# A graph kernel: counts rounded to 16 bits by GpSimd and turned as 16-bit blocks, and another order of VectorE's work behind attention

## The chip, the cores and the metric

The kernel runs on one core of a Trainium2 chip. The metric is the device time of one execution in microseconds; the median of several runs counts. Five engines work side by side, each through its own list of instructions: TensorE (PE in the profile, with its weight loads as PEld), VectorE (DVE), ScalarE (ACT), GpSimd (POOL) and SyncE (SP), which here only issues transfers. They wait for each other through semaphores.

## The reference

1250 nodes with 512 features, 21250 edges. Two layers, each behind a layer norm and a ReLU, each added to its input:

```
h = max(layernorm(x), 0);  x = x + attention(h)
h = max(layernorm(x), 0);  x = x + experts(h)

attention:  h = nodes @ W + b_w
            e = leaky_relu(s_dst[dst] + s_src[src] + b_a, 0.2);  w = exp(e)
            out[n] = sum over edges into n of w / (sum of w) * h[src]
experts:    gates = softmax(x @ gate_W + gate_b);  the top 2 of 4 experts of each node
            each expert: twice  h = relu((mean of h over neighbours) @ Wl + bl + h @ Wr)
            out = sum over the two of gate * expert output
```

## The kernel before

**Counts.** The graph is turned into a dense matrix of counts first: `CT[:, t, n]` (125 x 10 x 1250, 32-bit) says how many edges go from source node (t, p) to target node n. It is made on TensorE from one-hot rows in ten batches; `windows_out` copies it from PSUM. In the last layer of the experts the same counts are needed by target node, as 16-bit numbers in DRAM (`c_d`), from which GpSimd gathers rows. So the kernel turns every block of CT once.

**Attention.** It runs over `QN` = 5 blocks of 250 target nodes, and in each over `NP` = 5 pairs of the T = 10 source tiles; pair g = 5 q + j. For each pair VectorE makes the arguments (`arguments`, `z_l`), ScalarE the exponentials (`z_e`), VectorE multiplies them by the counts (`weights`, `p_f`), ScalarE copies the high part (`p_hi`), and VectorE adds `p_f` to the running sum (`sum_up`) and subtracts for the low part (`weights_low`, `p_lo`). RA = 3 pairs are in flight. TensorE takes each source tile s with six matmuls of 512 columns (two target tiles, three products of high and low parts, function `three`), and waits for `p_lo` ahead of each pair. At the end of a block `weight_sums` sums the weights, and VectorE's `attended` divides, adds the input and takes the row statistics. VectorE's order of instructions is written out by hand.

**Turning.** `turn_counts(q, r)`, r = 0 to 5, turns four, four and two blocks of 125 x 125 for each of the two target tiles, behind source tiles s = 2 to 7 of its block. ScalarE's `counts_out` copies the turned blocks as 16-bit numbers into `c_16`, with the row sums as a by-product (`deg_part`, the degrees), and SyncE stores `c_16`. A flag `beyond`, read into a register, says that a count may be over 2048; then the part that 16 bits lose is kept as well. With these inputs it is 0, and the parts under `If(beyond)` are skipped.

**Behind attention.** The second layer norm (`norm2`, `h2_f`), its split into `nat_hi` and `nat_lo`, its transposes (`turn2`, `h2T_hi`, `h2T_lo`), the gate logits, and `neighbours1`: the sum over neighbours, which for row tile t multiplies `CT_hi[:, t]` (a cast of CT) by the high and the low part of that tile. The first two row tiles have their high and low parts in `nat_a`. From t = 2 on TensorE waits for `nat_lo` of tile t, which `rows_low(t)` makes on VectorE.

**GpSimd** builds constants in the first 10 us and then has nothing to do until the second layer's neighbour sums are done.

Of the kernel before, what the change touches and what calls it, by code (L numbers as in the profile page):

```python
# [37 lines left out]
def gnn_kernel(nc, x, src, dst, W0, b_w, a_vec, b_a, gate_W, gate_b, Wl, bl, Wr, out):  # L38
# [37 lines left out]
    with ctx:  # L76
# [4 lines left out]
        def at(name, shape, dt, offset):  # L81
            return nc.alloc_sbuf_tensor_at(name, shape, dt, offset=origin + offset)
# [146 lines left out]
        nat_a = at("nat_a", [P, 2, 2, D], F32R, R3 + 30528)  # L229
        assert R3 + 30528 + 8192 <= R4  # L230
        ag1 = at("ag1", [P, 4, D], F32, R4 + 8192)
        c_nat = at("c_nat", [P, 2, N], F32, R3 + 20480)
        c_16 = at("c_16", [P, 2, N], F16, R3 + 10240)
        c_lo = at("c_lo", [P, 2, N], F16, R3 + 15264)


        slots = at("slots", [128, 2, 18432], F32R, 0)
# [72 lines left out]
        def signals(names, start=0):  # L310
            return [Signal(ctx.enter_context(nc.semaphore(n)), start) for n in names.split()]
# [3 lines left out]
            "pad_ready spark_ready edges_in x_in x_late_in w0_in vec_in small_in gw_in ct_out x2_out rest_in")  # L315

        c_turned, c_nat_ready = signals("c_turned c_nat_ready")
        LOW_READY, LOW_OUT = 2 * (N // Q), 16
        (c_out,) = signals("c_out", 64)

# [79 lines left out]

        def counts_beyond(eng):

            eng.wait_ge(*flag_ready(1))
# [3 lines left out]
            return beyond  # L407

        def apart(eng):

# [14 lines left out]
        QN = N // Q  # L425
        CONSTS = 8
        TURNS = (4, 4, 2)
        CUTS = (slice(0, 112), slice(112, P))
        AGG = ((0, 4, 3, 1, 2), (9, 8, 5, 6, 7))
        AGG_BANK = {0: 0, 1: 1, 2: 2, 3: 3, 4: 4, 9: 3, 8: 4, 5: 5, 6: 6, 7: 7}  # L430
# [27 lines left out]
        def _(sp):  # L458
# [18 lines left out]
            for q in range(QN):  # L477
                for i in range(2):
                    n = q * Q + i * P
                    sp.wait_ge(*c_nat_ready(6 * q + 3 * i + 3))  # L480
                    for m in CUTS:
                        sp.dma_start(c_d[n + m.start:n + m.stop, :], c_16[m, i, :]).then_inc(c_out.sem, 16)
                    with sp.If(beyond_sp):
                        if q == i == 0:
                            sp.wait_ge(*ct_out(LOW_OUT))
                        sp.wait_ge(*rest_ready(2 * q + i + 1))
                        for m in CUTS:
                            sp.dma_start(cl_d[n + m.start:n + m.stop, :], c_lo[m, i, :]).then_inc(ct_out.sem, 16)

            sp.wait_ge(*x2_ready(T))  # L490
            for m in CUTS:
# [70 lines left out]
        def _(pool):  # L562
# [43 lines left out]
            with pool.If(beyond):  # L606
                for q in range(QN):
                    for i in range(2):
                        pool.wait_ge(*c_nat_ready(6 * q + 3 * i + 3))
                        if q > 0:  # L610
                            pool.wait_ge(*ct_out(LOW_OUT, 64 * q))
                        g.tensor_tensor(c_lo[:, i, :], c_nat[:, i, :], c_16[:, i, :], ALU.subtract
                                        ).then_inc(rest_ready.sem, 1)
            with pool.If(beyond):
                pool.wait_ge(*ct_out(16))
# [88 lines left out]
        def _(act):  # L704
# [98 lines left out]
                bias_in(b)  # L803
                windows_out(b)

            beyond = counts_beyond(act)

            def row_out(k):
                act.wait_ge(*sd_spread(k + 1))
# [26 lines left out]
            def counts_out(q, r):  # L836
                n = TURNS[r % 3]
                act.wait_ge(*c_turned(q * 6 + r + 1))
                if r == 0 and q > 0:
                    act.wait_ge(*c_out(0, q * 64))  # L840
                to, turned = slice(r % 3 * 4 * P, (r % 3 * 4 + n) * P), ps[0:P, 6 + r % 2, 0:n * P]
                with act.If(beyond):
                    if r == 0 and q > 0:
                        act.wait_ge(*rest_ready(2 * q))
                    copy(c_nat[:, r // 3, to], turned)
                a.activation(c_16[:, r // 3, to], turned, ACT.Copy,
                             accum_out=deg_part[:, q * 6 + r:q * 6 + r + 1]).then_inc(c_nat_ready.sem, 1)

            def root(k, n):
                act.wait_ge(*var2_ready(k + 1))  # L850
# [11 lines left out]
            for g in range(NP * QN + 3):  # L862
                if g < NP * QN:
                    exponentials(g)
                if 1 <= g <= NP * QN:
                    weights_high(g - 1)
                if g == 1:
                    product_high(T - 1)
                if g in (2, 8):
                    row_out({2: 1, 8: 2}[g])  # L870
                for q in range(QN):
                    for r in range(6):
                        if NP * q + (r + 2) // 2 + 3 == g:
# [16 lines left out]
            for t in range(T):  # L890
                if t == 2:
                    act.wait_ge(*p_used(NP * QN))
                if t >= 2:
                    rows_high(t)
                if t == 3:
                    root(1, slice(T - 2, T))
                if t + 2 == 5:
# [139 lines left out]
        def _(dve):  # L1037
# [198 lines left out]
            dve.wait_ge(*flag_ready(1))  # L1236
            for b in range(T):
                tile_and_batch(b)
                if b == T - 1:
# [132 lines left out]
                    "p (c n) -> p c n", n=P), f32(h2T_hi[:, :, t * P:(t + 1) * P]), ALU.subtract  # L1372
                                ).then_inc(h2T_lo_ready.sem, 1)

            attended(QN - 1)
# [9 lines left out]
            def rows_low(t):  # L1385
                dve.wait_ge(*h2_hi_ready((t - 2) % T + 1))
                v.tensor_tensor(nat_lo[:, t, :], h2_f[:, t, :], f32(nat_hi[:, t, :]), ALU.subtract
                                ).then_inc(h2_lo_ready.sem, 1)
# [232 lines left out]
        def _(pe):  # L1621
# [165 lines left out]
            def turn_counts(q, r):  # L1787

                n = TURNS[r % 3]
                if q == 0 and r == 1:  # L1790
                    pe.wait_ge(*row_ready(2))
                pe.wait_ge(*c_nat_ready(q * 6 + max(r - 1, 0)))
                for k in range(n):
                    t = r % 3 * 4 + k
                    last = nc.tensor.transpose(ps[0:P, 6 + r % 2, k * P:(k + 1) * P],  # L1795
                                               CT[:, t, q * Q + r // 3 * P:q * Q + r // 3 * P + P], ident[0:P, 0:P])
                last.then_inc(c_turned.sem, 1)

            def weighted_sums(q):
                for j in range(NP):  # L1800
# [5 lines left out]
                    for m in range(2):  # L1806
# [85 lines left out]
            beyond = counts_beyond(pe)  # L1892
            turn2(0)
            turn2(1)
            for t in range(T):
# [194 lines left out]
```

## Time and profile before

| | |
|---|---|
| median of 3 runs | 774.83 us (774.81 to 775.18) |
| profiled execution | 777.36 us, span of the profile 775.3 us |
| PE busy | 745.5 us, 96% of the span |
| PEld, DVE, ACT, POOL busy | 605.7, 395.0, 278.9, 120.3 us |
| chain that ended last | PE 91%, DVE 5%, ACT 2%, issue 1% |

The stages: one-hot rows and counts to about 108 us, attention from 108 to 197, second layer norm and neighbour sums to 261, the experts' first layer to 488, and the second, for gathered rows, to the end. A row of a time line gives the start and the length in us, the engine, the line, the operation, what is written and read, how many instructions it covers, and in brackets the idle time before it and what ended it. The length of a pipelined instruction is longer than the step to the next one; steps between starts say what one costs in a stream.

### The profile page before, as it was taken

Reading aid. Unit: us, or ns where it says so; the run is one execution under the profiler, and the core shown is the slowest. Engines: PE = TensorE matmul, PEld = TensorE weight load, DVE = VectorE, ACT = ScalarE, POOL = GpSimd, SP = SyncE. Lnnn points to the kernel's source line nnn. Section 1 sums busy time; section 2 is a strip of 40 time slices with the busy share of each in tenths; the row PEclk is TensorE's granted clock in tenths of the full one; section 3 lists DMA queues with packets and bytes.
Section 4 is the critical chain, followed back from the end, with each engine's and each line's share of the span. In section 5 each row is a group of like instructions: output and inputs, shape, how many; then the busy total and the mean of one; then the engine's idle time right before and its main releaser. Section 6 shows DMA issues by size and latency. Waiting matters only on the chain.

```text
span 775.3 us, 11763 instructions
## 1 busy us (share of the span) xinstructions
PE 745.5 (96%) x3746; PEld 605.7 (78%) x3746; DVE 395.0 (51%) x979; ACT 278.9 (36%) x577; POOL 120.3 (16%) x133
## 2 busy tenths in 40 slices
PE   5899989999999999999999999899999999999994
PEld 3589968888788887777777777788887888888883
DVE  8898998997742549423525324333323323323320
ACT  6966675655543523312314213122122212211211
POOL 4000000000000103720000100231332322322211
PEclk9999999999999999999999999999999999999997
DMA  9000001111401447799696873599427944349800
GB/s 216 20 4 4 4 1 34 33 50 34 148 2 55 126 130 244 210 347 323 248 358 241 302 283 86 155 274 321 89 53 221 341 123 87 75 101 283 293 11 6
DMA packets 45319, 115.09 MB, mean 148 GB/s; under 512 B 7300, under 2 KB 7432, under 8 KB 45241
## 3 DMA queue, kind: packets, MB, share of 16 engines
q1 hardware_dynamic: 28581, 77.60, 30.7%
q0 software_dynamic: 8016, 19.59, 11.0%
q10 hardware_dynamic: 8644, 16.86, 6.5%
q8 instruction: 48, 0.79, 0.4%
q14 instruction: 30, 0.25, 0.1%
HBM read 64.85 MB, written 50.07 MB: 148 GB/s over the span
## 4 chain that ended last, share of the span: by engine, by line
PE 91%; DVE 5%; ACT 2%; issue 1%; POOL 0%; DVEq 0%; ACTq 0%; POOLq 0%
PE ps L1629 18%; PE ps L1630 18%; PE ps L1631 18%; PE ps L2021 7%; PE ps L2020 6%; PE ps L1706 3%; PE ps L1878 3%; PE ps L1879 3%; PE ps L1942 2%; PE ps L2031 1%; PE ps L1986 1%; PE ps L1795 1%; PE ps L1767 1%; PE ps L1657 1%; PE ps L1769 1%; PE ps L1768 1%
## 5 line engine op out<-in xcount | busy, mean ns | idle before, releaser
L2021 PE MATMUL ps<-slots,CTs 125*128 x230 | 91.2, 396 | 0.0
L2020 PE MATMUL ps<-slots,CTs 125*128 x207 | 81.5, 394 | 0.0
L1460 DVE TENSOR_TENSOR he_t<-ps,b_b 125x512 f32<-125x512 f32 x40 | 27.6, 691 | 102.5 <-PE ps L1631 70.9
L964 ACT ACTIVATE slots<-he_t 125x512 fp32r<-125x512 f32 x40 | 25.3, 635 | 148.4 <-DVE he_t L1460 141.6
L1553 DVE CAST CTs<-ps 125x512 fp32r<-125x512 f16 (+1 forms) x69 | 37.3, 595 | 76.5 <-PE ps L1942 72.8
L671 POOL DMA_INDIRECT out<-tg,rec x23 | 37.1, 1613 | 182.5 <-ACT tg L1014 159.0
L1629 PE MATMUL ps<-W,agT_hi 128*125 128x512 f32 x160 | 63.5, 397 | 0.0
L1629 PE MATMUL ps<-W,h2T_hi 128*125 128x512 f32 x160 | 63.4, 396 | 0.0
L1631 PE MATMUL ps<-W,agT_lo 128*125 128x512 f32 x160 | 63.3, 396 | 0.0
L1630 PE MATMUL ps<-W,agT_hi 128*125 128x512 f32 x160 | 63.2, 395 | 0.0
L1630 PE MATMUL ps<-W,h2T_hi 128*125 128x512 f32 x160 | 63.2, 395 | 0.0
L1631 PE MATMUL ps<-W,h2T_lo 128*125 128x512 f32 x160 | 63.1, 394 | 0.0
L1599 DVE TENSOR_TENSOR tm<-ps,b_b 128x512 f32<-128x512 f32 x23 | 15.9, 692 | 81.9 <-PE ps L1631 81.9
L1199 DVE TENSOR_SCALAR onehot_g<-iota_h,column 125x250 bf16<-125x250 f16 x250 | 49.7, 281 | 6.0 <-PE ps L1706 4.6
L1007 ACT ACTIVATE heT<-ps 128x512 fp32r<-128x512 f32 x23 | 13.8, 599 | 107.3 <-PE ps L1986 102.7
L2021 PEld LDWEIGHTS ps<-slots,CTs 125*128 125x128 f32 x230 | 43.3, 188 | 9.8
L2020 PEld LDWEIGHTS ps<-slots,CTs 125*128 125x128 f32 x207 | 38.9, 188 | 8.9
L1629 PE MATMUL ps<-nat_hi,p_hi 125*125 125x512 f32 x100 | 42.4, 424 | 2.4 <-issue 2.0
L1018 ACT ACTIVATE agn<-ps,rec 128x512 f32<-128x512 f32 x23 | 15.8, 688 | 79.4 <-PE ps L2021 79.4
L1629 PE MATMUL ps<-slots,heT 128*128 x92 | 40.0, 435 | 0.1
L1630 PE MATMUL ps<-nat_lo,p_hi 125*125 125x512 f32 x100 | 39.6, 396 | 0.0
L1631 PE MATMUL ps<-nat_hi,p_lo 125*125 125x512 f32 x100 | 39.5, 395 | 0.0
(299 smaller groups left out, 1666.9 us busy)
## 6 DMA issues: line engine op xcount, KB each, us to landing
he_d<-slots SPq DMA_DIRECT2D x30, 448.0 KB
slots<-he_d SPq DMA_DIRECT2D x30, 448.0 KB
w_d<-slots SPq DMA_DIRECT2D x3, 4096.0 KB, 17.4
slots<-w_d SPq DMA_DIRECT2D x24, 512.0 KB
t_d<-he_t SPq DMA_DIRECT2D x40, 224.0 KB
raw<-in_L_gnn_Wl ACTq DMA_DIRECT2D x4, 1024.0 KB, 9.0
raw<-in_L_gnn_Wr ACTq DMA_DIRECT2D x4, 1024.0 KB, 5.6
slots<-in_L_gnn_Wl ACTq DMA_DIRECT2D x4, 1024.0 KB, 10.0
```

The source lines that it names most:

```text
L671: g.indirect_dma_start(out, bass.IndirectOffsetOnAxis(ap=i32(rec[:, i, 2:3]), axis=0), tg[i % 3][:], None, bounds_check=N - 1, oob_is_err= ...
L964: a.activation(HE[:, t, 0:D], he_t[:, (x * T + t) % 4, :], ACT.Relu).then_inc(he_hi_ready.sem, 1)
L1199: last = v.tensor_scalar(onehot_g[:, k, j, :], iota_h[:], column[:, b % 2 * BW + k, j:j + 1], None, ALU.is_equal)
L1460: v.tensor_tensor(he_t[:, n % 4, :], ps[0:P, bank_of(x, g, t), :], b1_b[:, x % 2, :], ALU.add).then_inc(pre_ready.sem, 1)
L1553: v.tensor_copy(CTs[:, 4 * r:4 * r + n, :], turned_counts(r, n)).then_inc(cts_ready.sem, 1)
L1629: mm(o, l_hi, r_hi, start=start, stop=False)
L1630: mm(o, l_hi, r_lo, start=False, stop=False)
L1631: return mm(o, l_lo, r_hi, start=False, stop=stop)
L1706: last = mm(ps[0:P, k, 0:WT], onehot_p[:, bass.ds(first + j, 1), :].rearrange("p o n -> p (o n)"), onehot_g[:, slot, j, :], start=opens an ...
L1878: mm(o, count, hi, start=t == 0, stop=False)
L2020: mm(o, CTs[:, t, :], part(k, P, t * 1024, P), start=False, stop=False)
L2021: last = mm(o, CTs[:, t, :], part(k, P, t * 1024 + D, P), start=False, stop=t == T - 1)
```

## The change

GpSimd casts the counts of each block of 250 target nodes to 16 bits: `ct_16[q % 2]`, 125 x 10 x 250, once the counts are complete and the first layer's product of the last tile is done (the place in memory was that of the first layer's weights). Block q + 1 is cast after block q; from block 2 on the cast waits until the block that had its buffer is turned. It also casts a 16-bit identity, `ident_a`. TensorE turns the 16-bit blocks into 16-bit PSUM; ScalarE copies them to `c_16`. The 32-bit way stays for the case `beyond`, and a second flag, `usual`, selects the new way; TensorE and ScalarE read both into registers. In block 0 the turns move two source tiles back (`TURN_FROM`). Some tiles move in memory; the wait of ScalarE for the stored `c_16` moves one row tile back.

Behind attention VectorE makes the gate weights' low part, `CT_hi` and `nat_lo` of row tile 2 and `h2T_lo` of tile 1 ahead of the statistics of the last two tiles and of the degrees.

```diff
+        ct_16 = [at(f"ct_16_{k}", [P, T, Q], F16, R3 + 4096 + 5024 * k) for k in range(2)]
+        ident_a = at("ident_a", [P, P], F16, R2 + 39328)
...
+        TURN_FROM = (4, 2)
...
@@ GpSimd
+            pool.wait_ge(*batch_done(T))
+            g.tensor_copy(ident_a[:], ident[0:P, 0:P]).then_inc(consts.sem, 1)
+            pool.wait_ge(*window_out(NW))
+            pool.wait_ge(*hw_done(T))
+
+            def counts_16(q):
+                if q > 1:
+                    pool.wait_ge(*c_turned(6 * (q - 1)))
+                g.tensor_copy(ct_16[q % 2][:], CT[:, :, q * Q:(q + 1) * Q]).then_inc(ct_16_ready.sem, 1)
+
+            counts_16(0)
+            for q in range(QN):
+                if q + 1 < QN:
+                    counts_16(q + 1)
+                with pool.If(beyond):
...
@@ ScalarE, counts_out
-                a.activation(c_16[:, r // 3, to], turned, ACT.Copy,
-                             accum_out=deg_part[:, q * 6 + r:q * 6 + r + 1]).then_inc(c_nat_ready.sem, 1)
+                with act.If(usual):
+                    a.activation(c_16[:, r // 3, to].rearrange("p (t n) -> p t n", n=P),
+                                 ps_h[0:P, 6 + r % 2, 0:n * S].rearrange("p (t n) -> p t n", n=S)[:, :, 0:P], ACT.Copy,
+                                 accum_out=deg_part[:, q * 6 + r:q * 6 + r + 1]).then_inc(c_nat_ready.sem, 1)
...
-                        if NP * q + (r + 2) // 2 + 3 == g:
+                        if NP * q + (r + TURN_FROM[q > 0]) // 2 + 3 == g:
...
@@ VectorE
+            v.tensor_scalar(flag_i[:, 1:2], fl_f[:, 1:2], EXACT, None, ALU.is_le).then_inc(flag_ready.sem, 1)
...
             attended(QN - 1)
             turned_low2(0)
+            dve.wait_ge(*gw_hi_ready(1))
+            v.tensor_tensor(gw[:, :, NE:], gw_f[:], f32(gw[:, :, 0:NE]), ALU.subtract).then_inc(gw_lo_ready.sem, 1)
+            counts_high(2)
+            rows_low(2)
+            turned_low2(1)
             dve.wait_ge(*stats_ready(T))
             normed(1, late)
-            dve.wait_ge(*gw_hi_ready(1))
-            v.tensor_tensor(gw[:, :, NE:], gw_f[:], f32(gw[:, :, 0:NE]), ALU.subtract).then_inc(gw_lo_ready.sem, 1)
...
-            for t in range(T):
-                if t >= 2:
+            for t in range(1, T):
+                if t >= 3:
                     rows_low(t)
...
-                if t > 0:
+                if t > 1:
                     turned_low2(t)
...
@@ TensorE, turn_counts
+                if r == 0:
+                    pe.wait_ge(*ct_16_ready(q + 1))
...
+                with pe.If(usual):
+                    for k in range(n):
+                        t = r % 3 * 4 + k
+                        last = nc.tensor.transpose(ps_h[0:P, 6 + r % 2, k * S:k * S + P],
+                                                   ct_16[q % 2][:, t, r // 3 * P:(r // 3 + 1) * P], ident_a[:])
+                    last.then_inc(c_turned.sem, 1)
+                with pe.If(beyond):
...
-                        if T - 8 <= s < T - 2:
-                            turn_counts(q, s - (T - 8))
+                        if TURN_FROM[q > 0] <= s < TURN_FROM[q > 0] + 6:
+                            turn_counts(q, s - TURN_FROM[q > 0])
```

## Rows read from the trace of the kernel before

**Rows 1.** TensorE's waits from 100 to 330 us: us in all, times, longest.

```profile
PE ps L1629 <- issue: 2.0, 1, 2.0
PE ps L1878 <- DVE nat_lo L1387: 0.9, 1, 0.9
PE ps L1629 <- DVE p_lo L1313: 0.4, 1, 0.4
```

**Rows 2.** Time line of TensorE around a group of four 32-bit transposes, attention.

```profile
115.98 0.60 PE L1795 MATMUL ps<-ident,CT 125*125 125x125 f32 x4
...
116.66 0.40 PE L1630 MATMUL ps<-nat_lo,p_hi 125*125 125x512 f32 x1
116.89 0.39 PE L1631 MATMUL ps<-nat_hi,p_lo 125*125 125x512 f32 x1
```

**Rows 3.** The same around ten 16-bit transposes, last layer; a skipped conditional precedes them.

```profile
568.36 0.39 PE L2021 MATMUL ps<-slots,CTs 125*128 x1
568.59 0.74 PE L1942 MATMUL ps<-ident_h,crow 128*125 128x128 f16 x10
...
569.45 0.39 PE L1630 MATMUL ps<-slots,heT 128*128 x1
```

**Rows 4.** Time line of attention's last block, VectorE and TensorE.

```profile
186.14 0.68 DVE L1313 TENSOR_TENSOR p_lo<-p_f,p_hi 125x500 fp32r<-125x500 f32 x1
...
186.87 0.49 PE L1629 MATMUL ps<-nat_hi,p_hi 125*125 125x512 f32 x1
```

**Rows 5.** Time line of VectorE behind attention.

```profile
200.95 0.66 DVE L1371 TENSOR_TENSOR h2T_lo<-ps,h2T_hi 128x500 fp32r<-128x500 f32 x1
...
202.63 1.53 DVE L1358 CAST CT_hi<-CT 125x1250 fp32r<-125x1250 f32 x2
```

**Rows 6.** Stretches: length, busy us of PE, PEld, DVE, ACT, POOL, granted clock, DMA.

```profile
206.00:208.00 2.00, 2.00 (x7) 1.55 (x6) 1.97 (x6) 0.27 (x1) 0.00 (x0) 0.58 0.93 295
```

**Rows 7.** Time line of TensorE behind attention, rounds of row tiles 2 and 3.

```profile
203.82 0.65 PE L1839 MATMUL ps<-ident,h_f 125*128 125x125 f32 x4
205.40 0.50 PE L1878 MATMUL ps<-nat_hi,CT_hi 125*125 125x512 f32 x1 [0.94 <-DVE nat_lo L1387]
...
210.19 0.65 PE L1839 MATMUL ps<-ident,h_f 125*128 125x125 f32 x4
210.59 0.48 PE L1878 MATMUL ps<-nat_hi,CT_hi 125*125 125x512 f32 x1
...
213.79 0.64 PE L1839 MATMUL ps<-ident,h_f 125*128 125x125 f32 x4
```

**Rows 8.** GpSimd's groups of instructions by form: busy us, mean ns.

```profile
L600 POOL CAST iota_h<-iota_i 125x250 f16<-125x250 int32 x1 | 0.4, 394 | 0.1
...
L632 POOL CAST tile_f<-tile_i 125x24 f32<-125x24 int32 x1 | 0.2, 204 | 0.1
```

**Rows 9.** Time line of GpSimd and then VectorE at 262 us.

```profile
262.59 0.30 POOL L629 TENSOR_SCALAR_AFFINE_SELECT before_p<-before_p 125x125 f32<-125x125 f32 x1
...
262.59 0.31 DVE L1441 TENSOR_TENSOR cmp<-lg 125x10 f32<-125x10 f32 x1
...
263.23 0.18 DVE L1441 TENSOR_TENSOR cmp<-lg 125x10 f32<-125x10 f32 x1
```

**Rows 10.** Time line of VectorE and then GpSimd at 7 us.

```profile
6.69 0.93 DVE L1067 SCALAR_TENSOR_TENSOR e_q<-e_t,e_src 32x750 fp32r<-32x750 f32 x1
...
7.08 0.63 POOL L593 TENSOR_SCALAR_AFFINE_SELECT tri<-tri 50x50 f32<-50x50 f32 x1
```

**Rows 11.** Time line of VectorE at attention's start.

```profile
108.32 0.68 DVE L1294 SCALAR_TENSOR_TENSOR p_f<-z_e,CT 125x500 f32<-125x500 f32 x1 [0.27 <-ACT z_e L824]
```

**Rows 12.** A stretch of one block of attention, columns as in rows 6.

```profile
146.34:163.34 17.00, 17.00 (x89) 14.18 (x89) 15.45 (x32) 10.03 (x27) 0.00 (x0) 1.00 0.12 37
```

**Rows 13.** Time line of block 2, VectorE and TensorE.

```profile
151.40 0.67 DVE L1313 TENSOR_TENSOR p_lo<-p_f,p_hi 125x500 fp32r<-125x500 f32 x1
...
152.59 0.48 PE L1629 MATMUL ps<-nat_hi,p_hi 125*125 125x512 f32 x1
```

More of the change, by code:

```diff
@@ L228, in gnn_kernel @@
         rest = at("rest", [P, T, P], F32R, row_at)
-        nat_a = at("nat_a", [P, 2, 2, D], F32R, R3 + 30528)
-        assert R3 + 30528 + 8192 <= R4
+        nat_a = at("nat_a", [P, 2, 2, D], F32R, R3 + 31808)
+        assert R3 + 31808 + 8192 <= R4
         ag1 = at("ag1", [P, 4, D], F32, R4 + 8192)
-        c_nat = at("c_nat", [P, 2, N], F32, R3 + 20480)
-        c_16 = at("c_16", [P, 2, N], F16, R3 + 10240)
-        c_lo = at("c_lo", [P, 2, N], F16, R3 + 15264)
+        c_nat = at("c_nat", [P, 2, N], F32, R3 + 21760)
+        ct_16 = [at(f"ct_16_{k}", [P, T, Q], F16, R3 + 4096 + 5024 * k) for k in range(2)]
+        c_16 = at("c_16", [P, 2, N], F16, R3 + 14144)
+        c_lo = at("c_lo", [P, N], F16, R3 + 19168)
+        ident_a = at("ident_a", [P, P], F16, R2 + 39328)
         slots = at("slots", [128, 2, 18432], F32R, 0)
@@ L317, in gnn_kernel @@
         c_turned, c_nat_ready = signals("c_turned c_nat_ready")
+        (ct_16_ready,) = signals("ct_16_ready")
         LOW_READY, LOW_OUT = 2 * (N // Q), 16
@@ L401, in counts_beyond @@
         def counts_beyond(eng):
-            eng.wait_ge(*flag_ready(1))
+            eng.wait_ge(*flag_ready(2))
             _, (beyond,) = nc.values_load_multi_w_load_instructions(
@@ L407, in counts_beyond, with counts_within @@
             return beyond
+        def counts_within(eng):
+            eng.wait_ge(*flag_ready(2))
+            _, (usual,) = nc.values_load_multi_w_load_instructions(
+                flag_i[0:1, 1:2], engines=[eng.engine], min_val=0, max_val=1,
+                skip_runtime_bounds_check_because="it is 0 or 1")
+            return usual
         def apart(eng):
@@ L487, in _ @@
                         for m in CUTS:
-                            sp.dma_start(cl_d[n + m.start:n + m.stop, :], c_lo[m, i, :]).then_inc(ct_out.sem, 16)
+                            sp.dma_start(cl_d[n + m.start:n + m.stop, :], c_lo[m, :]).then_inc(ct_out.sem, 16)
             sp.wait_ge(*x2_ready(T))
@@ L605, in _ @@
             beyond = counts_beyond(pool)
-            with pool.If(beyond):
-                for q in range(QN):
+            pool.wait_ge(*batch_done(T))
[11 more added lines that the diff above has]
+                with pool.If(beyond):
                     for i in range(2):
                         pool.wait_ge(*c_nat_ready(6 * q + 3 * i + 3))
-                        if q > 0:
-                            pool.wait_ge(*ct_out(LOW_OUT, 64 * q))
-                        g.tensor_tensor(c_lo[:, i, :], c_nat[:, i, :], c_16[:, i, :], ALU.subtract
+                        if q + i > 0:
+                            pool.wait_ge(*ct_out(LOW_OUT, 64 * q + 32 * i))
+                        g.tensor_tensor(c_lo[:], c_nat[:, i, :], c_16[:, i, :], ALU.subtract
                                         ).then_inc(rest_ready.sem, 1)
@@ L804, in _ @@
                 windows_out(b)
-            beyond = counts_beyond(act)
+            beyond, usual = counts_beyond(act), counts_within(act)
             def row_out(k):
@@ L845, in counts_out @@
                     copy(c_nat[:, r // 3, to], turned)
-                a.activation(c_16[:, r // 3, to], turned, ACT.Copy,
-                             accum_out=deg_part[:, q * 6 + r:q * 6 + r + 1]).then_inc(c_nat_ready.sem, 1)
+                    a.activation(c_16[:, r // 3, to], turned, ACT.Copy,
+                                 accum_out=deg_part[:, q * 6 + r:q * 6 + r + 1]).then_inc(c_nat_ready.sem, 1)
+                with act.If(usual):
+                    a.activation(c_16[:, r // 3, to].rearrange("p (t n) -> p t n", n=P),
+                                 ps_h[0:P, 6 + r % 2, 0:n * S].rearrange("p (t n) -> p t n", n=S)[:, :, 0:P], ACT.Copy,
+                                 accum_out=deg_part[:, q * 6 + r:q * 6 + r + 1]).then_inc(c_nat_ready.sem, 1)
             def root(k, n):
@@ L896, in _ @@
                     root(1, slice(T - 2, T))
-                if t + 2 == 5:
+                if t + 2 == 6:
                     act.wait_ge(*c_out(64 * QN))
@@ L1234, in spread_out @@
                                 ).then_inc(sd_ready.sem, 1)
-            dve.wait_ge(*flag_ready(1))
+            dve.wait_ge(*flag_ready(2))
             for b in range(T):
@@ L1373, in turned_low2, with rows_low @@
                                 ).then_inc(h2T_lo_ready.sem, 1)
+            def rows_low(t):
+                dve.wait_ge(*h2_hi_ready((t - 2) % T + 1))
+                v.tensor_tensor(nat_lo[:, t, :], h2_f[:, t, :], f32(nat_hi[:, t, :]), ALU.subtract
+                                ).then_inc(h2_lo_ready.sem, 1)
             attended(QN - 1)
             turned_low2(0)
+            dve.wait_ge(*gw_hi_ready(1))
[3 more added lines that the diff above has]
+            turned_low2(1)
             dve.wait_ge(*stats_ready(T))
             normed(1, late)
-            dve.wait_ge(*gw_hi_ready(1))
-            v.tensor_tensor(gw[:, :, NE:], gw_f[:], f32(gw[:, :, 0:NE]), ALU.subtract).then_inc(gw_lo_ready.sem, 1)
             dve.wait_ge(*c_nat_ready(6 * QN))
@@ L1384, in _ @@
             link(v.reciprocal(inv_deg[:], inv_deg[:]))
[L1385 to L1388, printed above, removed]
-            for t in range(T):
-                if t >= 2:
+            for t in range(1, T):
+                if t >= 3:
                     rows_low(t)
@@ L1792, in turn_counts @@
                 pe.wait_ge(*c_nat_ready(q * 6 + max(r - 1, 0)))
[L1793 to L1797, printed above, removed]
+                if r == 0:
+                    pe.wait_ge(*ct_16_ready(q + 1))
+                    if q == 0:
+                        pe.wait_ge(*consts(CONSTS + 1))
+                with pe.If(usual):
[5 more added lines that the diff above has]
+                with pe.If(beyond):
+                    for k in range(n):
+                        t = r % 3 * 4 + k
+                        last = nc.tensor.transpose(ps[0:P, 6 + r % 2, k * P:(k + 1) * P],
+                                                   CT[:, t, q * Q + r // 3 * P:q * Q + r // 3 * P + P], ident[0:P, 0:P])
+                    last.then_inc(c_turned.sem, 1)
             def weighted_sums(q):
@@ L1815, in weighted_sums @@
                             last.then_inc(p_used.sem, 1)
-                        if T - 8 <= s < T - 2:
-                            turn_counts(q, s - (T - 8))
+                        if TURN_FROM[q > 0] <= s < TURN_FROM[q > 0] + 6:
+                            turn_counts(q, s - TURN_FROM[q > 0])
+            beyond, usual = counts_beyond(pe), counts_within(pe)
             pe.wait_ge(*window_out(NW))
@@ L1890, in turn_means1 @@
                 last.then_inc(ag1_turned.sem, 1)
-            beyond = counts_beyond(pe)
             turn2(0)
```

## The prediction

> **What bounds the kernel now.** I read the page's busy shares first, then TensorE's list of waits, then the time line around the change. TensorE is the bound: from 100 to 330 us it waits three times, 3.3 us in all [rows 1]: 2.0 us before attention's first product (the weights of the first source tiles are not ready), 0.4 us before the second pair of source tiles, and 0.9 us for the third row tile's low part (`nat_lo`). So what leaves TensorE's stream there comes off the end, and what makes VectorE late at one of these places goes onto it. Behind 330 us its stream has almost no gaps, and its loads are triggered by its own progress; I take it that it shifts as a whole.
>
> **Part 1, the 100 transposes.** Attention turns 20 blocks of counts in each of five blocks of target nodes. A group of four 32-bit transposes starts at 115.98, and the second matmul behind it at 116.66, where one matmul steps by 0.23: 0.68 - 0.23 = 0.45 us, 112 ns each [rows 2]. Ten 16-bit transposes of nearly the same shape, in the last layer: 569.45 - 568.59 - 0.23 = 0.63 us, 63 ns each [rows 3]. I take 48 ns saved (bounds: 37, if entering a group costs 0.08 us of the 0.63 and groups of four and two pay it as often as they come, and 55, if it costs nothing and 125 columns are cheaper than 128), so 0.95 us per block and 4.75 in all. Two groups of four in the last block give nothing: there TensorE already waits for VectorE (the low part ends at 186.82, the product starts at 186.87) [rows 4]; that is 8 x 0.048 = 0.4 less. ScalarE gets one more conditional between a turned block and its copy, on the chain that leads to the second layer norm; I take 0.15 us there (0 to 0.5). Sum: -4.2 us.
>
> The conditionals on TensorE, two per group, I cost at nothing: one stands just ahead of the ten transposes at 568.59, and the step over it is the usual 0.23 [rows 3]. Their cover is the queue of matmuls before them. The two registers that TensorE now reads before attention lie in its 2 us wait, and ScalarE's lies beside its copies of the last windows.
>
> **Part 2, VectorE's new order.** The sequence after attention is h2T_lo of tile 0, statistics, gate weights, degrees, two `CT_hi`, h2T_lo of tile 1, `nat_lo` of tile 2. The first of these ends at about 201.6, and two casts, 0.77 us each, start at 202.63 [rows 5], so 1.0 us of small work, a second cast and an h2T_lo (0.66) stood ahead of `nat_lo`. In the new order only the gate weights, one cast and `nat_lo` stand there: 201.6 + 0.1 + 0.8 + 0.7 = 203.2. TensorE's transposes start at 203.82, and it goes on 0.4 later, as from 210.19 to 210.59 [rows 7], so it needs it at 204.2. The 0.94 us wait goes. The moved work is late for nobody: the degrees are used only by the means at this stage's end, the square root of the last two tiles waits on ScalarE behind other work anyway, and row tile 3's low part, followed through the new order in the same way, comes 0.5 us before its need.
> The wait has a second price. The granted clock was 0.58 from 206 to 208 [rows 6], that is half speed (1.2 GHz) for most of it, after the pause; and one round, from one set of transposes to the next, took 210.19 - 203.82 = 6.37 us where the next took 213.79 - 210.19 = 3.60 [rows 7]. Both together are 2.8 us. I take all of it: other rounds have the same small matmuls without the wait and keep their clock. Bound: 0.9 if the clock falls anyway.
>
> **Part 3, GpSimd's five casts and VectorE.** Before, GpSimd does nothing in this stage. Now it casts 125 x 2500 numbers five times. Length: 24 columns took 0.204 us and 250 took 0.394 [rows 8], 0.84 ns a column, so 0.18 + 2500 x 0.00084 = 2.3 us; the upper bound is ten casts of 250, 3.9 us. The first cast ends by 111.2, and TensorE needs it behind 30 matmuls of block 0, 7 us after it starts on them: it doesn't wait for it.
> VectorE does. At 262.59 GpSimd's select (0.30 us, reading SBUF) and VectorE's 10-column comparison of two SBUF inputs start together; the comparison takes 0.31 and ends when the select ends, where the same one takes 0.18 at 263.23 [rows 9]. And at 7.08 a GpSimd select of 50 columns, behind a VectorE instruction with two SBUF inputs that runs to 7.62, takes 0.63 [rows 10]; GpSimd gets in behind that one instruction, though VectorE has more to do. So each shuts the other out, and GpSimd gets its turn. All of attention's VectorE work but the normalisation of finished rows has two SBUF inputs. The rows show this only for operations of 0.3 us. The lower bound is no hold beyond that, 5 x 0.13 = 0.7 us, the upper one the whole length; I take the whole length, since in both pairs the held one ended only when the other did.
> The Trainium skill (SBUF — State Buffer, Who interferes with whom) says that a VectorE instruction with two SBUF inputs and a GpSimd one that reads SBUF exclude each other for the whole instruction. The rows agree, for short ones. By that rule the sum is the one below; by what the rows show of duration alone, it would be the lower bound's.
>
> Where it lands: (a) the start. Casts 0 and 1 follow each other once the last product is out, at about 108.3, just as VectorE starts its first weights [rows 11] in the chain that TensorE waits for. One VectorE instruction may slip between them; the chain is 2 x 2.25 = 4.5 us later, and so is TensorE's first product. It has then been idle for 2.0 + 4.5 = 6.5 us. After the 0.94 us pause it went to half speed, after the 2.0 us one not; I take it that it does here. The low clock cost 2.8 - 0.94 = 1.8 us of the one round at most; here 0.4 of it is free, in the wait for the second pair of tiles. I take 0.9 (0 to 1.4). Start: +5.4 us (0.5 to 5.9 at this cast length).
> (b) Cast 2 waits for block 0's last turn; VectorE then has only normalisation to do, which reads PSUM: 0.
> (c) Casts 3 and 4 start after the last turn of blocks 1 and 2, when VectorE isn't through. It is busy 15.45 us of a block's 17.0 [rows 12]; with a block of 16.05 there are 0.6 us left, so it comes 2.3 - 0.6 = 1.7 us late to the next block. The low part of its third pair of tiles was done at about 152.0, TensorE took them up at 152.59 [rows 13]: a cushion of 0.6, less the 8 x 0.048 = 0.4 by which TensorE now comes earlier. TensorE waits 1.7 - 0.2 = 1.5 us, twice: +2.9. What is queued behind VectorE's held instruction is the sum and low part of the last pair and then the next block's normalisation; TensorE waits for none of them, but for what follows.
> The small cast of the identity (0.3 us, near 104) costs VectorE up to 0.25 us that its wait for `row` at 106 covers.
>
> **Sum.** -4.2 - 2.8 + 5.4 + 2.9 = +1.3 us. The profiled execution took 777.36 us over a span of 775.3; it would become 778.7 and 776.6. The median of the three runs is 774.83, 2.5 less, and the change is added to that: 776.1.
>
> **Rivals.**
> - *They share.* GpSimd holds VectorE for about half of its length (bursts, or it yields). Start 2.5, blocks 0.5: -7.0 + 3.0 = -4.0, 770.8 us. For it: no row shows a hold over 0.3 us. Against: the held one always ended with the holder.
> - *No hold worth speaking of.* -7.0 and at most +0.7: 768.1 us. Against it: the two pairs of rows.
> - *Slower, by one thing: a longer cast.* Ten separate rows of 250 at 3.9 us. Start 2 x 3.85 + 0.9 = 8.6, blocks 2 x (3.9 - 0.6 - 0.2) = 6.2, less 7.0: +7.8, 782.6 us. Each 0.1 us of a cast costs 0.4 us; above 2.4 us the change is slower by more than can be told from nothing. For it: GpSimd's own rows are of 250 columns at most. Against: its time grows evenly with the columns.
> - *The new order gives only 0.9*, since the clock falls anyway: +1.9 on any of these. The rounds after it speak against it.
>
> **How the numbers follow.** A measurement of this kernel can tell about 0.2%, 1.55 us, from no change. The full hold has 0.55, and gives 776.1 with its own range of 773.5 to 778.5; of this, slower 0.24, same 0.29, faster 0.02. Sharing has 0.25 (faster 0.21, same 0.04), no hold 0.12 (faster), the longer cast 0.08 (slower). Together: faster 0.35, same 0.33, slower 0.32. The range leaves out the 0.12 below and the longer cast above: 769.5 to 779.0.
>
> **What the profile after would show.** The 100 transposes in groups of 0.25 us instead of 0.45; no wait for `nat_lo` and a granted clock of 1.00 from 206 to 210; GpSimd's casts of 2.3 us with VectorE starting nothing with two SBUF inputs beside them; TensorE's wait before attention 6.5 instead of 2.0 us, and new waits for `p_lo` of some 1.5 us in blocks 2 and 3. The prediction is wrong if VectorE's instructions run beside the casts, if a cast takes far from 2.3 us, or if TensorE's wait at the start is still 2 us.

## The result: 777.5 us, 0.3% slower

The changed kernel took 777.47 us (median of 8 runs, 776.97 to 777.59), the kernel before beside it 774.87 us (8 runs, 774.24 to 775.98). The ratio is 1.0031, 95% interval 1.0020 to 1.0041: slower by 2.4 us by the ratio and by 2.6 us by the medians, and clear of no change. Forecast were 776.1 us and a range from 769.5 to 779.0. The profiled execution took 777.35 us over a span of 775.2.

TensorE's waits from 100 to 330 us in the changed kernel (against [rows 1]):

```profile
PE ps L1662 <- issue: 6.1, 1, 6.1
PE ps L1662 <- DVE p_lo L1343: 1.7, 3, 0.8
```

The wait at the start has grown from 2.0 to 6.1 us, those for `p_lo` from 0.4 to 1.7, and the wait for `nat_lo` is gone. Who makes the start late stands in the time lines of GpSimd, VectorE and TensorE at attention's start (against [rows 8] and [rows 11]):

```profile
108.37 5.21 POOL L626 CAST ct<-CT 125x2500 f16<-125x2500 f32 x2 [3.91 <-PE ps L1802]
...
108.36 0.68 DVE L1324 SCALAR_TENSOR_TENSOR p_f<-z_e,CT 125x500 f32<-125x500 f32 x1 [0.26 <-ACT z_e L849]
108.95 4.89 DVE L1307 SCALAR_TENSOR_TENSOR z_l<-row,s_rest,row_low 125x250 f32<-125x250 f32 x2
113.77 0.67 DVE L1324 SCALAR_TENSOR_TENSOR p_f<-z_e,CT 125x500 f32<-125x500 f32 x1
...
115.13 0.76 PE L1662 MATMUL ps<-nat_hi,p_hi 125*125 125x512 f32 x1 [6.06 <-issue]
115.69 0.63 PE L1663 MATMUL ps<-nat_lo,p_hi 125*125 125x512 f32 x1
```

In the kernel before the same two `z_l` are:

```profile
108.92 0.86 DVE L1277 SCALAR_TENSOR_TENSOR z_l<-row,s_rest,row_low 125x250 f32<-125x250 f32 x2
```

They take 4.89 us beside two casts instead of 0.86, 4.03 us more. By VectorE's list of that tile one `z_l` took 2.50 us at most and 0.47 in the median: each of the two is held by one cast, and the first slips in before the second cast. TensorE then runs at half speed (a matmul of 512 columns steps by 0.42 us instead of 0.23; the granted clock is 0.50 from 116 to 117 us).

The 16-bit transposes in TensorE's stream, a group of four and one of two (against [rows 2]):

```profile
123.78 0.39 PE L1833 MATMUL ps<-ident_a,ct 125*125 125x125 f16 x4
123.98 0.47 PE L1662 MATMUL ps<-nat_hi,p_hi 125*125 125x512 f32 x1
124.29 0.39 PE L1663 MATMUL ps<-nat_lo,p_hi 125*125 125x512 f32 x1
...
127.14 0.28 PE L1833 MATMUL ps<-ident_a,ct 125*125 125x125 f16 x2
127.22 0.48 PE L1662 MATMUL ps<-nat_hi,p_hi 125*125 125x512 f32 x1
127.54 0.40 PE L1663 MATMUL ps<-nat_lo,p_hi 125*125 125x512 f32 x1
```

By the reckoning of [rows 2]: 124.29 - 123.78 - 0.23 = 0.28 us for four, 0.17 for two. Four were 0.45. VectorE beside block 3's cast (146.32 to 148.94 us), the two waits of TensorE behind such casts, and the stretch from block 1's denominators to block 2's (against [rows 12]):

```profile
146.32 2.88 DVE L1307 SCALAR_TENSOR_TENSOR z_l<-row,s_rest,row_low 125x250 f32<-125x250 f32 x2
...
156.67 0.50 PE L1662 MATMUL ps<-nat_hi,p_hi 125*125 125x512 f32 x1 [0.59 <-DVE p_lo L1343]
...
173.95 0.50 PE L1662 MATMUL ps<-nat_hi,p_hi 125*125 125x512 f32 x1 [0.78 <-DVE p_lo L1343]
```

```profile
148.95:166.02 17.07, 16.48 (x89) 13.23 (x88) 17.00 (x32) 10.14 (x27) 2.41 (x1) 1.00 0.12 38
```

VectorE is busy for 17.00 of 17.07 us, where it had 1.55 us of slack. The stretch holds block 4's cast (2.41 us), so part of the 17.00 is time in which VectorE is held. Behind attention, the place of [rows 7] and of [rows 6]:

```profile
207.26 0.65 PE L1884 MATMUL ps<-ident,h_f 125*128 125x125 f32 x4
207.67 0.48 PE L1923 MATMUL ps<-nat_hi,CT_hi 125*125 125x512 f32 x1
...
210.86 0.65 PE L1884 MATMUL ps<-ident,h_f 125*128 125x125 f32 x4
```

```profile
206.00:208.00 2.00, 2.00 (x17) 1.85 (x16) 1.90 (x9) 0.05 (x1) 0.00 (x0) 1.00 1.00 317
```

One round takes 3.60 us, no wait, full clock, as forecast. Yet the profiled spans of the two kernels are equal (775.3 and 775.2), and the medians are 2.6 us apart. So before any cause is named, the first profile of the kernel before has to be looked at again.

### The profile page after: what moved, and what is told of

The parts are those of the page before. It is cut to its first block, busy times and chain, and to the rows that moved or that the text cites. A ratio compares the mean times of both kernels' runs of the same rounds, so it can differ in the third digit from the quotient of the medians.

```text
span 775.2 us, 11871 instructions
## 1 busy us (share of the span) xinstructions
PE 741.5 (96%) x3746; PEld 601.6 (78%) x3746; DVE 402.3 (52%) x980; ACT 278.9 (36%) x577; POOL 133.6 (17%) x139
## 4 chain that ended last, share of the span: by engine, by line
PE 90%; DVE 6%; issue 2%; ACT 1%; POOL 0%; DVEq 0%; ACTq 0%; POOLq 0%
PE ps L1662 18%; PE ps L1663 17%; PE ps L1664 17%; PE ps L2065 7%; PE ps L2064 6%; PE ps L1739 3%; PE ps L1923 3%; PE ps L1924 3%; PE ps L1986 2%; PE ps L2075 1%; PE ps L2030 1%; PE ps L1800 1%; PE ps L1802 1%; PE ps L1801 1%; PE ps L1690 1%
## 5 line engine op out<-in xcount | busy, mean ns | idle before, releaser
L681 POOL DMA_INDIRECT crow<-c_d,rec x23 | 22.7, 985 | 103.1 <-DVE W L1461 96.4
```

## The experiments

All are measured against the kernel before on the same chip. The casts are numbered 0 to 4 by the block whose counts they make.

### The kernel before, once more

> The kernel before, once more, for its profile. The first profile of it lasted 777.36 us where its runs have a median of 774.9. Theory one: the low granted clock behind attention (206 to 210 us there, some 1.8 us) isn't in most executions, so this profile has a span of about 773 us and a granted clock of 1.00 from 206 to 208. Theory two: the episode is in every execution, and the 2.5 us lie elsewhere: span 773 us too, but with the episode. Ratio to itself 1.000.

774.69 us against 774.54, ratio 1.0009 (0.9998 to 1.0020). That is the resolution. The new profile has a span of 772.8 us, 2.5 less than the first one. Its stretches at 206 and at 495 us, then those of the first profile:

```profile
206.00:208.00 2.00, 2.00 (x12) 1.62 (x11) 1.97 (x6) 0.32 (x1) 0.00 (x0) 1.00 0.94 294
495.00:500.00 5.00, 5.00 (x16) 3.75 (x16) 0.78 (x2) 0.60 (x1) 2.59 (x3) 0.66 0.77 211
```

```profile
495.00:500.00 5.00, 3.44 (x11) 2.82 (x11) 0.69 (x1) 0.58 (x1) 3.82 (x4) 0.66 0.75 217
```

It waits 0.9 us for `nat_lo` as well, but the clock stays at 1.00 behind it. The half speed at 206 us was that execution's and doesn't come with every execution of the kernel. Of the 2.5 us between the two profiles 1.6 lie there, and 0.9 behind 495 us (by the marks explained in the next experiment).

### VectorE's new order alone

```diff
+            counts_high(2)
+            rows_low(2)
+            turned_low2(1)
             dve.wait_ge(*stats_ready(T))
             normed(1, late)
...
-            for t in range(T):
-                if t >= 2:
+            for t in range(1, T):
+                if t >= 3:
```

> The kernel before with VectorE's new order behind attention alone. By the prediction's term 2.8 us faster (ratio 0.9964), with no wait for nat_lo. If most executions of the kernel before have no episode of low clock, only the wait of 0.9 us is gained (0.9988).

772.17 us, ratio 0.9969 (0.9958 to 0.9980): 2.4 us faster. The wait for `nat_lo` is gone, and the stretch at 495 us, which was at 0.66 in both profiles of the kernel before, is at full clock:

```profile
495.00:500.00 5.00, 4.89 (x24) 3.65 (x23) 2.21 (x4) 0.60 (x1) 1.73 (x2) 1.00 0.79 220
```

Two marks in TensorE's time line separate the two effects: the denominators of the last block (the last group of eight `ones,p_sum` matmuls), and the first matmul behind TensorE's 1.6 us wait for `aggT` near 495 us. In the second profile of the kernel before, and then here:

```profile
196.61 0.93 PE L1783 MATMUL ps<-ones,p_sum 125*125 125x2 f32 x8
...
203.75 0.65 PE L1839 MATMUL ps<-ident,h_f 125*128 125x125 f32 x4
205.35 0.49 PE L1878 MATMUL ps<-nat_hi,CT_hi 125*125 125x512 f32 x1 [0.95 <-DVE nat_lo L1387]
...
494.93 0.58 PE L1629 MATMUL ps<-slots,aggT 128*128 x1 [1.61 <-DVE aggT L1589]
```

```profile
196.65 0.93 PE L1786 MATMUL ps<-ones,p_sum 125*125 125x2 f32 x8
...
203.79 0.65 PE L1842 MATMUL ps<-ident,h_f 125*128 125x125 f32 x4
204.19 0.48 PE L1881 MATMUL ps<-nat_hi,CT_hi 125*125 125x512 f32 x1
...
493.76 0.49 PE L1632 MATMUL ps<-slots,aggT 128*128 x1 [1.61 <-DVE aggT L1592]
```

From the first mark to the second it is 298.32 us in the second profile of the kernel before and 297.11 here: the order gives 1.2 us (2.8 against the first profile, 299.89). That is the wait alone: from the transposes to the product behind them it is 1.60 us with it and 0.40 without. The 0.95 in brackets counts only from the modelled end of the four pipelined transposes. From the second mark to the end of the span it is 277.87 and 276.44: another 1.4 us, from the clock and not from the order's own work.

### The change with VectorE's old order

```diff
-            counts_high(2)
-            rows_low(2)
-            turned_low2(1)
...
-            for t in range(1, T):
-                if t >= 3:
+            for t in range(T):
+                if t >= 2:
```

> The changed kernel with VectorE's old order: the 16-bit casts and turns alone. Theory hold (GpSimd's casts shut VectorE out for their length): the start costs 4.1 + 0.9, blocks 2 and 3 some 1.4, the turns give 3.5: +3 to +3.5 us, ratio 1.004 to 1.0045. Rival (the casts cost nothing, the new conditionals, register loads and waits do): the same time, so this run only gives the size.

777.65 us, ratio 1.0047 (1.0035 to 1.0059). The changed kernel's 777.47 is only 0.2 us less; by the ratios to the kernel before beside each it is 1.2 us less, and the two intervals touch. So the total times don't settle what the order gives here. The marks of the two profiles do: between the two marks the old order takes 298.55 us where the changed kernel takes 297.16, so the order gives 1.4 here too. From the second mark to the end it takes 276.55 where the changed kernel takes 277.96: the low clock at 497 us, which the changed kernel has (0.75 from 495 to 500) and this one hasn't, takes the 1.4 back.

### The change with the casts replaced by fills

```diff
-                g.tensor_copy(ct_16[q % 2][:], CT[:, :, q * Q:(q + 1) * Q]).then_inc(ct_16_ready.sem, 1)
+                g.memset(ct_16[q % 2][:], 0.0).then_inc(ct_16_ready.sem, 1)
```

> The changed kernel with each of GpSimd's five casts of the counts replaced by a fill with zeros of the same size (left out: the counts in 16 bits, so the second layer sums nothing); all waits, conditionals and 16-bit turns stay. Theory hold, with the condition that GpSimd reads SBUF: VectorE runs beside the fills, TensorE's wait before attention is 2 us again and there is no wait for p_lo in blocks 2 and 3: about 6 us less than the changed kernel, 771.5 us, ratio 0.9955. Rival one, any GpSimd work that long shuts VectorE out: ratio as the changed kernel's, 1.003. Rival two, conditionals, register loads and waits make the cost: 1.003 as well, but with VectorE not held.

769.19 us, ratio 0.9934 (0.9920 to 0.9949), 2.3 us better than expected. Of this 1.4 us are the clock near 495 us, which is up here and which the expectation left out; most of the rest is that the casts' reading cost 6.7 us and not 6. GpSimd, then VectorE and TensorE's waits:

```profile
108.39 4.31 POOL L626 MEMSET ct<- 125x2500 f16 x2 [3.92 <-PE ps L1802]
```

```profile
108.97 0.86 DVE L1307 SCALAR_TENSOR_TENSOR z_l<-row,s_rest,row_low 125x250 f32<-125x250 f32 x2
```

```profile
PE ps L1662 <- issue: 2.0, 1, 2.0
...
PE ps L1662 <- DVE p_lo L1343: 0.7, 2, 0.4
```

GpSimd is busy in the same places and for nearly as long (4.31 us for two fills, 5.21 for two casts), it writes the same tile, and VectorE isn't held. So the price lies in what a cast does and a fill doesn't, the reading of SBUF, not in GpSimd being busy, and not in the conditionals and registers, which are all still there.

### Casts 1 to 4 where VectorE reads PSUM

```diff
             def counts_16(q):
+                if q > 0:
+                    pool.wait_ge(*den_done(q))
                 if q > 1:
                     pool.wait_ge(*c_turned(6 * (q - 1)))
```

> The changed kernel, with casts 1 to 4 moved behind the denominators of the block before them, where VectorE's next work (attended) reads PSUM; cast 0 stays at the start. If GpSimd holds VectorE only while both read two SBUF operands, only one cast lies beside VectorE's low parts at the start: the first product waits about 4.0 us instead of 6.1 (2.0 in the kernel before), the waits for p_lo of 0.6 to 0.8 us in blocks 2 and 3 go, and nothing new comes. Against the kernel before: 2.0 for the start, 0 to 1.0 for a lower clock after it, five blocks of transposes at 0.78 less (3.9), and 0.9 to 2.4 less for VectorE's order: 2.3 to 4.3 us faster, ratio 0.9945 to 0.997, the likeliest 0.996. If a cast holds VectorE whatever it reads, the hold moves into attended, at some 0.6 to 2.3 us a block for three blocks, and the ratio is 0.998 to 1.003. If the casts' place doesn't matter (only their sum), the ratio stays at the changed kernel's 1.003.

772.15 us, ratio 0.9969 (0.9957 to 0.9980): 2.4 to 2.6 us faster, at the low end of what was expected. GpSimd, VectorE and TensorE's wait at the start and at the second cast:

```profile
108.37 2.80 POOL L628 CAST ct<-CT 125x2500 f16<-125x2500 f32 x1 [3.92 <-PE ps L1804]
131.33 2.28 POOL L628 CAST ct<-CT 125x2500 f16<-125x2500 f32 x1 [20.16 <-PE ps L1818]
```

```profile
108.96 2.88 DVE L1309 SCALAR_TENSOR_TENSOR z_l<-row,s_rest,row_low 125x250 f32<-125x250 f32 x2
...
131.70 1.41 DVE L1294 SCALAR_TENSOR_TENSOR xs<-ps,rden,xs 125x512 f32<-125x512 f32 x2
133.02 1.28 DVE L1298 BATCH_NORM_STATS2 x_stats<-xs 125x6 f32<-125x512 f32 x2
```

```profile
PE ps L1664 <- issue: 4.0, 1, 4.0
...
PE ps L1664 <- DVE p_lo L1345: 0.3, 1, 0.3
```

One cast at the start costs TensorE 2.0 us, half of what two cost, and the waits in the blocks are gone. The normalisation `xs`, which has one operand in PSUM, runs wholly beside the second cast and takes 1.41 us; in the changed kernel at 151.28 us it takes 1.41 with no cast beside it. The statistics behind it lie beside the cast for 0.6 us only (1.28 and 1.27 us). The four casts behind the denominators cost nothing that shows: block 4's denominators come 2.64 us later than with the fills, and 2.63 of it is there at block 0's. Where a cast stands decides what it costs.

### Block 0 left at 32 bits, so that no cast stands at the start

```diff
-            counts_16(0)
             for q in range(QN):
                 if q + 1 < QN:
                     counts_16(q + 1)
...
+                        if q == 0:
+                            last = nc.tensor.transpose(ps[0:P, 6 + r % 2, k * P:(k + 1) * P],
+                                                       CT[:, t, r // 3 * P:r // 3 * P + P], ident[0:P, 0:P])
```

(added to the experiment above; ScalarE's copy of block 0 and the place of its turns are those of the kernel before)

> The kernel before with VectorE's new order, and 16-bit counts for blocks 1 to 4 alone: block 0 is turned as 32-bit, so that there is no cast at the start, and casts 1 to 4 stand behind the denominators. By the theory of the shared port no cast lies beside VectorE's two-operand work: TensorE waits 2.0 us for its first product as in the kernel before, four blocks of transposes give 0.78 us each (3.1), VectorE's order 0.9 to 2.4: 4.0 to 5.5 us faster, ratio 0.993 to 0.995, the best of all with the counts computed. If a cast holds VectorE wherever it stands, four casts cost 0.6 to 2.3 us each and the ratio is 0.996 to 1.004. If the gain of the 16-bit transposes is only apparent (something behind them waits anyway), the ratio is that of the new order alone, 0.997.

770.72 us, ratio 0.9943 (0.9927 to 0.9958): 4.1 to 4.4 us faster than the kernel before, 6.8 faster than the change. TensorE's wait at the start is 2.0 us again, and the longest `z_l` 0.48. It beats both kernels; its interval touches that of the new order alone (772.17 us), but at the end of attention's last block it is ahead of it, 194.90 against 196.65 us. It is so although the clock was 0.72 from 110 to 116 us here, which made block 0 end 0.9 us later; blocks 1 to 4 together are 2.7 us shorter.

### Every cast twice

```diff
                 g.tensor_copy(ct_16[q % 2][:], CT[:, :, q * Q:(q + 1) * Q]).then_inc(ct_16_ready.sem, 1)
+                pool.wait_ge(*ct_16_ready(2 * q + 1))
+                g.tensor_copy(ct_16[q % 2][:], CT[:, :, q * Q:(q + 1) * Q]).then_inc(ct_16_ready.sem, 1)
...
-                    pe.wait_ge(*ct_16_ready(q + 1))
+                    pe.wait_ge(*ct_16_ready(2 * q + 2))
```

> The changed kernel with every one of GpSimd's five casts made twice over: the same values, and nothing else changed. In the changed kernel two casts at the start lengthened VectorE's low part by 4.0 us, and each of casts 3 and 4 by 2.0 us, of which TensorE waited 0.6 and 0.8 us since VectorE had some slack there. If one cast holds VectorE's two-operand work for 2.0 us each time, the start grows by 4.0 us (TensorE's wait for issue from 6.1 to 10.1 us), casts 3 to 5 grow TensorE's waits by about 2.0 us each (the slack is used up), and cast 2, whose repeat runs out of the stretch in which VectorE reads PSUM, costs up to 0.7 us: some 10.7 us slower than the changed kernel, 788 us, ratio to the kernel before 1.017. If VectorE and GpSimd rather share the port as it comes (a repeat finds a port half used), the start grows by 2 us and the blocks by 1 us each: 782 us, ratio 1.010. If only the first use matters (starting the cast), the ratio stays near 1.004.

("Casts 3 to 5" was a slip of numbering: only casts 3 and 4 lie beside two-operand work in this way, and the sum of 10.7 had one wait too many.) 788.76 us, ratio 1.0167 (1.0136 to 1.0198), 11.3 us above the changed kernel. VectorE at the start, and TensorE's waits:

```profile
108.96 4.89 DVE L1309 SCALAR_TENSOR_TENSOR z_l<-row,s_rest,row_low 125x250 f32<-125x250 f32 x2
113.78 2.74 DVE L1326 SCALAR_TENSOR_TENSOR p_f<-z_e,CT 125x500 f32<-125x500 f32 x1
...
116.44 2.74 DVE L1345 TENSOR_TENSOR p_lo<-p_f,p_hi 125x500 fp32r<-125x500 f32 x1
```

```profile
PE ps L1664 <- issue: 10.2, 1, 10.2
...
PE ps L1664 <- DVE p_lo L1345: 4.9, 4, 2.1
```

The start is as forecast: four casts, four VectorE instructions of about 2 us more each, and 10.2 us of waiting. In the blocks the total is near and its parts are not: the waits for `p_lo` grew by 3.2 us, and TensorE's clock fell behind them (0.87 from 165 to 175 us, 0.86 from 185 to 196), for which the expectation had nothing. By the denominators, blocks 2 and 3 grew by 3.8 and 3.1 us (20.88 and 20.39 instead of 17.07 and 17.26), where 2.0 was written for each. Block 1, with cast 2 and its repeat, grew by 0.3, where up to 0.7 was expected. That the sum came out near is partly luck.

### The changed kernel and the last but one, profiled again

> The changed kernel again, for a second profile of it. If TensorE's lower clock behind a pause belongs to the kernel's order of work, the granted clock is again near 0.65 at 110 to 116 us and 0.75 at 495 to 500 us. If it depends on the execution, one of the two stretches shows 1.00.

777.43 us, span 775.3. The clock is 0.69 from 110 to 116 us and 0.80 from 495 to 500: both are there again.

> The kernel of the last run (16-bit counts for blocks 1 to 4 alone) again, for a second profile. Its first one showed the clock at 0.72 in the stretch from 110 to 116 us behind a pause of 2.0 us, where the kernel before, with the same pause, kept 1.00 in two profiles. If that depends on the execution, this profile may show 1.00 there and a span shorter by about 1.2 us; if it belongs to the kernel, 0.72 again.

771.34 us, span 769.5. The clock keeps 1.00 from 110 to 116 us this time, behind the same wait of 2.0 us, but it fell elsewhere (0.83 from 40 to 50 us, where the first profile had 1.00), and everything behind that came 1.4 us later. Where the clock falls thus varies between executions of one kernel as well; the span is 0.7 longer, not 1.2 shorter.

## Why the forecast was right, and which terms were off

The places and the mechanism held: GpSimd's casts hold VectorE at the start and in blocks 2 and 3, and this eats more than the transposes and the order give. Three terms were too large. The costs were overstated by 1.6 us and the gains by 2.6, so the errors cancelled in good part, and that the total came within 1.4 us is partly luck, the sign too: the forecast gains less the measured cost (-7.0 + 6.7) would have been -0.3 us, no change that can be told. TensorE's time line at each block's denominators gives the account (us; start of the group of eight `ones,p_sum`; then the times between the marks of the experiments):

| kernel | block 0 | 1 | 2 | 3 | 4 | from block 4's to `aggT` | from `aggT` to the end |
|---|---|---|---|---|---|---|---|
| before, second profile | 128.27 | 145.32 | 162.32 | 179.37 | 196.61 | 298.32 | 277.87 |
| changed | 132.65 | 148.95 | 166.02 | 183.28 | 200.08 | 297.16 | 277.96 |
| changed, old order | 132.68 | 148.97 | 166.08 | 183.30 | 200.10 | 298.55 | 276.55 |
| changed, fills | 127.70 | 144.00 | 160.30 | 176.56 | 193.36 | 297.12 | 276.52 |
| order alone | 128.30 | 145.35 | 162.35 | 179.40 | 196.65 | 297.11 | 276.44 |
| casts 1 to 4 beside PSUM work | 130.33 | 146.63 | 162.93 | 179.20 | 196.00 | 297.08 | 276.92 |
| block 0 at 32 bits | 129.22 | 145.52 | 161.82 | 178.09 | 194.90 | 297.12 | 276.78 |
| casts twice | 137.01 | 153.58 | 174.46 | 194.85 | 211.66 | 297.11 | 278.13 |

**Part 1, forecast -4.2: it gives -3.25.** The kernel with fills has everything but the casts' reading, and reaches the end of block 4 at 193.36 instead of 196.61. A full block takes 16.30 instead of 17.05 us, 0.75 for 20 transposes, 37 ns each. That is the lower bound of the forecast: its condition was that entering a group costs something. The groups of four and of two at 0.28 and 0.17 us say the same: 0.055 us for each transpose and 0.06 for the group. The 32-bit ones show no such part: 0.45 us for four and 0.22 for two (in the kernel before, at 119.64 us). A price read from a group of ten [rows 3] was carried to groups of four and two with only part of its fixed cost. The conditionals are in this sum as well, and leave it no room to be dear; ScalarE's one wasn't measured by itself.

**Part 2, forecast -2.8: it gives -1.2 to -1.4.** Here the step failed that adds the two halves: "Both together are 2.8 us. I take all of it". The wait is there in both profiles and goes, and is worth 1.2 us by the steps, where the 0.94 in brackets was taken; the round at half speed [rows 6, 7] was in the first of the two profiles only. Against that profile the order does give 2.78 (299.89 to 297.11). The forecast said itself that the profiled execution was 2.5 us above the median, but it made its sum from that execution's rows and added it to the median. A loss that made the profile longer than the median can't be saved from the median. No new wait shows for the moved work, as forecast. What was in no sum is the clock at 497 us: with the order alone it stays up, and the measured gain was 2.4 us; in the changed kernel it falls, and the order's gain is undone there.

**Part 3, forecast +8.3: it costs 6.7** (200.08 - 193.36). The start, forecast +5.4, is 132.65 - 127.70 = +4.95: 4.03 of chain, where 4.5 stood, and 0.9 left over, which fits the stretch at half speed, as forecast. Cast 2 costs nothing, as forecast. Casts 3 and 4, forecast +2.9, cost (166.02 - 148.95) - 16.30 = 0.77 and (183.28 - 166.02) - 16.26 = 1.00, 1.8 together. The terms that were off are the hold, which makes VectorE 2.0 us late where the cast's whole 2.3 was taken (part of the cast lies beside a VectorE instruction already on its way: that is argued from the rows, not tested), and the block's length: since a transpose gives 37 and not 48 ns, a block is 16.30 us and not 16.05, and VectorE's 15.5 us of work leave 0.8 of slack, not 0.6. A hold of 2.0, less 0.8 of slack, less 0.2 of cushion [rows 13] is 1.0, against 0.77 and 1.00. The length of a cast alone, forecast at 2.3 us from two short casts [rows 8], was 2.28; beside VectorE's work it was 2.4 to 2.8.
The hold was shown by three runs: fills of nearly the same length hold nothing, casts beside PSUM work hold nothing, and doubled casts double the hold. The Trainium skill (SBUF — State Buffer, Who interferes with whom) has this as an exclusive lock for the whole instruction; these runs agree with it for casts of 2.3 us, where the rows of the kernel before reached only 0.3.

**The sum** with the measured terms, against the second profile of the kernel before: -3.25 + 6.72 - 1.16 + 0.09 = +2.4 us, which is the difference of the spans, 775.2 - 772.8. Forecast was +1.3; parts 1 and 2 were too favourable by 2.6, part 3 too dear by 1.6.

**The rivals.** Sharing (770.8 us) falls with the doubled casts, which cost the full hold again, and a longer cast (782.6) with the 2.28 us. "No hold" (768.1) is what the kernel with fills shows: 769.2. "The new order gives only 0.9" was near in size (1.2 to 1.4) for the wrong reason: it had the clock fall at 206 us with either order, and in the second profile, of an execution close to the median (774.6 us), it doesn't fall there at all.

**Open.** Why the clock falls behind one pause and not behind another of the same length isn't settled; no run was made to steer it.

## What to carry to other kernels

Before work is given to an idle GpSimd, look at what VectorE does beside it. In these runs each cast that reads SBUF, put beside such work, stopped one VectorE instruction with two SBUF operands for about 2 us. Such a cast belongs beside VectorE's PSUM work, or nowhere on a critical start. The five casts cost 6.7 us where they fell; four of them, put behind one more wait, cost next to nothing. And when a profiled execution is longer than the median, find out first what made it so: what only that execution lost isn't there to be won.

## What the runs showed of the hardware

- TensorE's wait for `aggT` near 495 us is 1.6 us long in all eleven profiles. Where it ended at 494.9, 496.6, 497.2, 497.5 and 508.8 us, the clock fell behind it, and from there to the end it was 277.8 to 278.7 us; where it ended at 490.5, 492.0, 492.6, 493.1, 493.8 and 498.7 us, it didn't, and it was 276.4 to 277.0. Profiles whose wait ended one or two microseconds apart thus fell on different sides; whether that shift or something else decides isn't shown. Of the order's 2.4 us, 1.4 came that way; in this kernel an effect below 1.5 us can't be read from the total time alone, but it can from two marks in the time line. The Trainium skill (TensorE: Matmul & The Clock Gate, The HAM clock gate) says that the same kernel shows different numbers of slow matmuls from run to run, counted from its start. The pairs of profiles here agree that it varies, and show it behind waits in the middle, of 0.9 us at 205 and of 2.0 us at 111.
- GpSimd and VectorE took turns strictly, instruction by instruction: four casts in a row held four VectorE instructions in a row, one each (4.89 for two, 2.74, 2.74 us).
- GpSimd's cast of the identity, 125 x 125, took 0.73 us from 103.73 us on, where 0.3 was forecast, and where a cast of 128 x 128 took 0.30 later in the same run. VectorE was in its two `diag` then, of two SBUF inputs each (103.62, 1.36 us for both, 1.27 in the kernel before). That looks like the same hold in the other direction. So does the first cast of the kernel with casts 1 to 4 beside PSUM work: it started 0.01 us behind a `p_f` of 0.68 us and took 2.80, where the others took 2.28, and two fills in the same place took 4.31, no more than twice one of them. No run tested this direction by itself.
- A GpSimd fill of 125 x 2500 16-bit numbers takes 2.18 us, hardly less than the cast that also reads (2.28).
